# Products of state index 0 scaled on ScalarE instead of VectorE in a selective-scan decoder layer

## The chip, the cores and the metric

The kernel runs on one core of one Trainium2 chip. The metric is the device time of one execution in microseconds, the median of several runs. A core has TensorE (PE: matmuls and transposes into the eight PSUM banks, with PEld for its weight loads), VectorE (DVE), ScalarE (ACT), GpSimd (POOL), and SyncE (SP), which issues the DMAs. Each engine runs its own list of instructions in order and waits on semaphores for the others.

## What is computed

A decoder layer in float32 on 16 sequences of 128 tokens and 1024 features: a selective-scan block, a linear cross-attention and a gated low-rank expert layer, each with residual and layer norm. The change touches the scan alone:

```python
dt = softplus(ts @ W_dt.T + b_dt)
A = -exp(A_log)                              # (2048, 16)
def step(state, inp):
    dt_t, B_t, C_t, u_t = inp
    dA = exp(dt_t[..., None] * A)
    state = state * dA + (dt_t * u_t)[..., None] * B_t[:, None, :]
    y = einsum('bdn,bn->bd', state, C_t)     # sum over the 16 state indices
    return state, y
...
y = ys + x * D
y = y * silu(gate)
return y @ W_out.T
```

## The kernel before

**Tiling.** The 2048 channels are 16 tiles of 128; four sequences (512 tokens) are one group. A step s, of 16, covers one group and a quarter of the channels (4 tiles); q = s % 4 is the quarter. Inside a step the loop runs over the 16 state indices n; U = 16 s + n numbers the units.

**One unit.** GpSimd multiplies dt*u by the row of B of index n into `hb[n % 4]` (L1056). ScalarE writes exp(dt*A) into bank 0 or 1, one tile at a time (L908); for tile i it waits until the scan two tiles earlier has freed that bank. VectorE scans each tile with it (L1143). TensorE transposes the states, four 128x128 pieces for each sequence b (L509, `turn(b)`): sequences 0 and 2 go to bank 2, 1 and 3 to bank 3. Then each bank is multiplied by the column of C (`cg[:, b, n]`) and added to `acc[:, b]`. For sequences 0 to 2 VectorE does this from PSUM in one instruction (`dve_acc`, L1158), or for n=0 as a plain scaled copy (L1155). Sequence 3 goes by ScalarE: a scaled copy (`act_part`, L761), into `acc` for n=0 and into `part` for the other n, where GpSimd adds it (L1013).

**Order.** It is written out by hand. TensorE does for each n: turn 0, turn 1, a share of the filler (projections of Z and X, L432, output products, L456, dt, L444; three 512-column products, each two passes in the trace), turn 2, turn 3, another share. At n=1 and n=11 a product of the next projection into bank 2 (`pe_ssm`, L469) stands behind the third sum. The step ends with transposes of `acc` (L542). VectorE does for each n: sums 0 and 1 of index n, scans 0 and 1 of index n+2, sum 2, scans 2 and 3 of index n+2, then a few odd pieces (`dve_between`); steps 5, 9 and 13 have layer-norm statistics (L1177) there at n=0. At a step's end come the skip and gate products (L1252, L1263), and in steps 4, 8 and 12 then the copy of C's columns into `cg` (L1235). ScalarE does for each n its four exps, with odd pieces between (`act_between`), and then the part of index n-2.

A turn waits until its bank has been read: turns 0, 2 and 3 on `acc_ok` (VectorE's count), turn 1 on `part_ok`.

Of the kernel before, what the change touches and what calls it, by code (L numbers as in the profile page):

```python
# [18 lines left out]
ALU = mybir.AluOpType  # L19
ACT = mybir.ActivationFunctionType  # L20
# [29 lines left out]
OWN = GB - 1  # L50
# [12 lines left out]
def has_x(s):  # L63
    return 0 <= s and LEAD + QD * s < NG * DT
# [29 lines left out]
x_mm conv_base conv_tap conv_done sx_exp sx_ln sx_ok u_ok u_stored0 u_stored1 u_stored2  # L94
ss_mm ss_added ss_square ss_sum ss_mean ss_ln ss_rstd ss_normed bt_mm bt_rows b_stored
wdt_loaded wo_loaded u_loaded0 u_loaded1 r_loaded brep_loaded0 brep_loaded1 brep_loaded2 brep_loaded3
dt_mm dt_abs dt_exp dt_ln dt_ok dtu_ok cg_ok exp_ok bm_ok scan_ok t_done acc_ok part_ok sum_ok yt_mm fin1 fin
z_mm z_copied z_exp z_ln z_sig z_ok o_mm r_added ln_stats ln_aggr ln_eps ln_rstd ln_ok x1_stored
p2_const ones_set ph_mm ph_ok gs_ok cn_loaded ct_loaded x1_loaded xres_loaded out_stored
k_mm k_max k_neg k_exp et_mm et_ok g_mm g_ok rk1 rk2 mt_mm mt_ok  # L100
# [5 lines left out]
def program(nc, a, out):  # L106
# [4 lines left out]
    with ExitStack() as ctx:  # L111
        def sb(name, shape):
            return ctx.enter_context(nc.sbuf_tensor(name, shape, F32))

        S = {name: ctx.enter_context(nc.semaphore(name)) for name in SEMS}

        def after(eng, name, count):

            if count > 0:
                eng.wait_ge(S[name], count)  # L120
# [20 lines left out]
        acc = at(32768, GB, QD * P)  # L141
# [7 lines left out]
        part = at(43520, 2, QD * P)  # L149
# [41 lines left out]
        cg = sb("cg", [P, GB, N])  # L191
# [14 lines left out]
        def bank(i):  # L206
            return banks[i // 2][:, (i % 2) * HALF:(i % 2 + 1) * HALF]
# [289 lines left out]
        def pe_step(pe, s):  # L497
            g, q = divmod(s, NQ)
            for n in range(N):
                U = N * s + n  # L500

                def turn(b):

                    if b == 1:
                        after(pe, "part_ok", U)
                    else:
                        after(pe, "acc_ok", OWN * U + (0, 0, 1, 2)[b])
                    for i in range(QD):
                        last = nc.tensor.transpose(bank(2 + b % 2)[:, i * P:(i + 1) * P],  # L509
                                                   hb[n % 4][:, i * GT + b * P:i * GT + (b + 1) * P],  # L510
                                                   ident[:, :])
                    last.then_inc(S["t_done"], 1)

                pe.wait_ge(S["scan_ok"], QD * (U + 1))
                if n == 2 and (has_x(s - 1) or s == 0):
                    pe.wait_ge(S["ss_added"], (LEAD + QD * s) // 2)
                if n == 4 and q == NQ - 1 and s + 1 < NS:
                    pe.wait_ge(S["bt_rows"], g + 2)
                if n == 12 and has_x(s):
                    pe.wait_ge(S["ss_added"], (LEAD + QD * s) // 2 + 1)  # L520
                turn(0)
                turn(1)
                pe_filler(pe, s, 2 * n)
                turn(2)
                turn(3)
                if n == 1 and (has_x(s - 1) or s == 0):
                    pe.wait_ge(S["acc_ok"], OWN * (U + 1))
                    pe_ssm(pe, (LEAD + QD * s) // 2 - 1)
                if n == 3 and q == NQ - 1 and s + 1 < NS:
                    pe.wait_ge(S["acc_ok"], OWN * (U + 1))  # L530
                    pe_rows(pe, g + 1)
                if n == 11 and has_x(s):
                    pe.wait_ge(S["acc_ok"], OWN * (U + 1))
                    pe_ssm(pe, (LEAD + QD * s) // 2)
                pe_filler(pe, s, 2 * n + 1)

            pe.wait_ge(S["acc_ok"], OWN * N * (s + 1))
            pe.wait_ge(S["sum_ok"], (N - 1) * (s + 1))
            for i in range(QD):
                pe_room(pe, "Y", QD * s + i)  # L540
                for b in range(GB):
                    last = nc.tensor.transpose(home("Y", QD * s + i)[:, b * P:(b + 1) * P],  # L542
                                               acc[:, b, i * P:(i + 1) * P], ident[:, :])
                last.then_inc(S["yt_mm"], 1)
# [200 lines left out]
        def act_ss(act, g):  # L745
# [2 lines left out]
            act.wait_ge(S["ss_ln"], g + 1)  # L748
            nc.scalar.activation(ss3[:, :, :], ss3[:, :, :], ACT.Exp, scale=-0.5).then_inc(S["ss_rstd"], 1)

        def act_part(act, s, n):

            act.wait_ge(S["t_done"], QD * (N * s + n + 1))
            if n == 0:
                after(act, "yt_mm", QD * s)
                act.wait_ge(S["cg_ok"], s // NQ + 1)
                dst = acc[:, OWN, :]
            else:
                after(act, "sum_ok", (N - 1) * s + max(n - 2, 0))
                dst = part[:, n % 2, :]  # L760
            nc.scalar.activation(dst, bank(3), ACT.Identity, scale=cg[:, OWN, n:n + 1])\  # L761
                .then_inc(S["part_ok"], 1)

        def act_between(act, s, n, slot):
# [134 lines left out]
        def act_step(act, s):  # L899
            q = s % NQ  # L900
            for n in range(N):
                U = N * s + n
                for i in range(QD):
                    if n == 0:
                        act.wait_ge(S["dt_ok"], QD * s + i + 1)

                    after(act, "scan_ok", QD * U + i - 1)
                    nc.scalar.activation(by_seq(bank(i % 2))[:, :, 1:SEQ],  # L908
                                         by_seq(dt[s % 2][:, i, :])[:, :, 1:SEQ], ACT.Exp,
                                         scale=a_sb[:, QD * q + i, n:n + 1]).then_inc(S["exp_ok"], 1)  # L910
                    act_between(act, s, n, i)
                if U >= 2:
                    act_part(act, (U - 2) // N, (U - 2) % N)

        def act_keys(act, b, o):
# [90 lines left out]
        def pool_sums(pool, s, n):  # L1006

            if n == 0:
                return
            pool.wait_ge(S["part_ok"], N * s + n + 1)  # L1010
            after(pool, "sum_ok", (N - 1) * s + n - 1)
            v = acc[:, OWN, :]
            nc.gpsimd.tensor_tensor(v, v, part[:, n % 2, :], ALU.add).then_inc(S["sum_ok"], 1)  # L1013
# [131 lines left out]

        def dve_acc(dve, s, n, b):

            k = OWN * (N * s + n) + b
            dve.wait_ge(S["t_done"], QD * (N * s + n) + b + 1)
            c = cg[:, b, n:n + 1]  # L1150
            if n == 0:
                if b == 0:
                    after(dve, "yt_mm", QD * s)
                    dve.wait_ge(S["cg_ok"], s // NQ + 1)
                last = nc.vector.tensor_scalar(acc[:, b, :], bank(2 + b % 2), c, None, ALU.mult)  # L1155
            else:
                dve.wait_ge(S["acc_ok"], k - OWN + 1)
                last = nc.vector.scalar_tensor_tensor(acc[:, b, :], bank(2 + b % 2), c, acc[:, b, :],  # L1158
                                                      ALU.mult, ALU.add)
            last.then_inc(S["acc_ok"], 1)  # L1160

        def dve_out(dve, s, c):

# [66 lines left out]

        def dve_step(dve, s):
            if s % NQ == 0:
                after(dve, "acc_ok", OWN * N * s)
                after(dve, "part_ok", N * s)
                nc.vector.tensor_copy(cg[:, :, :], ssn[:, :, R + N:SS]).then_inc(S["cg_ok"], 1)  # L1235
            for n in range(N):
                U = N * s + n

                for part in range(2):
                    for b in range(2 * part, min(2 * part + 2, OWN)):  # L1240
                        dve_acc(dve, s, n, b)
                    if U + 2 < N * NS:
                        for i in (2 * part, 2 * part + 1):
                            dve_scan(dve, U + 2, i)
                dve_between(dve, s, n)
            if s > 0:
                dve_out(dve, s, 7)

            def skip(i):
                dve.wait_ge(S["yt_mm"], QD * s + i + 1)  # L1250
                d = QD * (s % NQ) + i
                nc.vector.scalar_tensor_tensor(yq[:, i, :], uq[s % 2][:, i, :], dsk[:, d:d + 1],  # L1252
                                               home("Y", QD * s + i), ALU.mult, ALU.add)\
                    .then_inc(S["fin1"], 1)

            after(dve, "o_mm", 8 * s)
            skip(0)
            for i in range(QD):
# [432 lines left out]
```

## Time and profile before

| | |
|---|---|
| median of 3 runs | 3166.69 us (3164.89 to 3166.74) |
| profiled execution | 3165.11 us, span of its instructions 3163.1 us |
| TensorE busy | 2777.4 us (88%) |
| VectorE busy | 2691.1 us (85%) |
| ScalarE busy | 1629.4 us (52%) |
| GpSimd busy | 1850.6 us (59%) |
| mean granted TensorE clock | 0.943 of 2.4 GHz |

Busy shares are means over the whole span. The steps run from about 200 to 2347 us, and the attention and expert part from there to the end. In the rows, a bracket behind a row is the time for which the engine sat idle before it and what released it. A row of a timeline may merge several instructions of one kind.

### The profile page before, as it was taken

What the parts mean: (1) busy time and instruction counts of PE and PEld (TensorE: products, weight loads), DVE (VectorE), ACT (ScalarE), POOL (GpSimd) and SP (SyncE); (2) the same over time, 40 slices, a digit from 0 to 9 for tenths busy, and PEclk for the clock granted to TensorE, in tenths of its full rate; (3) what the DMA queues carried; (4) which work ended last, traced back from release to release, by engine and by line L of the source; (5) the groups of instructions that cost most, each with busy time, mean ns of one, the idle gap of its engine ahead of it and who ended that gap; (6) DMA issues with size and microseconds to landing.
All of it is one profiled execution on the core that took longest, in us unless ns stands there. A gap on an engine that the chain in (4) does not pass through costs nothing.

```text
span 3163.1 us, 34709 instructions
## 1 busy us (share of the span) xinstructions
PE 2777.4 (88%) x10928; PEld 1569.8 (50%) x10928; DVE 2691.1 (85%) x3630; ACT 1629.4 (52%) x2698; POOL 1850.6 (59%) x820
## 2 busy tenths in 40 slices
PE   8967889899978998998988788778887999999996
PEld 4434555455545555554555445444544555555553
DVE  2369999999999999999999999999974877877785
ACT  2346556465545646564555555446533555555553
POOL 1169778687857777785877688678841212221221
PEclk9988999999989999999999898888988999999998
DMA  5442333333242342424233231422202211111110
GB/s 170 131 106 75 100 94 102 118 106 107 89 139 80 102 131 78 126 82 142 80 102 103 63 108 61 128 88 74 67 14 87 73 60 60 53 60 60 60 54 26
DMA packets 132872, 281.27 MB, mean 89 GB/s; under 512 B 12528, under 2 KB 12656, under 8 KB 132224
## 3 DMA queue, kind: packets, MB, share of 16 engines
q1 hardware_dynamic: 132736, 279.59, 28.8%
q8 instruction: 70, 1.15, 0.1%
q14 instruction: 66, 0.54, 0.1%
HBM read 245.86 MB, written 33.69 MB: 88 GB/s over the span
## 4 chain that ended last, share of the span: by engine, by line
PE 49%; DVE 37%; issue 11%; ACT 1%; DMA 0%; POOL 0%; DVEq 0%; SPq 0%; POOLq 0%; ACTq 0%
DVE arena L1143 19%; PE banks L432 15%; DVE arena L1158 8%; PE banks L456 6%; PE banks L509 6%; PE banks L597 3%; PE banks L640 3%; PE banks L553 3%; PE banks L578 3%; PE banks L608 2%; PE banks L469 2%; PE banks L568 1%; DVE arena L1086 1%; DVE rbuf L1171 1%; DVE arena L1252 1%
## 5 line engine op out<-in xcount | busy, mean ns | idle before, releaser
L1056 POOL TENSOR_TENSOR arena<-arena 128x2048 f32<-128x2048 f32 x256 | 1162.8, 4543 | 97.2 <-PE banks L509 97.1
L1143 DVE TENSOR_TENSOR_SCAN arena<-banks,arena 128x512 f32<-128x512 f32 x1024 | 1190.0, 1202 | 9.5 <-POOL arena L1056 9.2
L908 ACT ACTIVATE banks<-arena,a_sb 128x508 f32<-128x508 f32 x1024 | 700.8, 684 | 924.7 <-DVE arena L1143 924.2
L432 PE MATMUL banks<-arena 128*128 128x512 f32 x2048 | 970.2, 613 | 12.3 <-DMA arena<-in_xT 8.1
L509 PE MATMUL banks<-ident,arena 128*128 128x128 f32 x4096 | 593.1, 290 | 214.4 <-DVE arena L1158 134.8
L509 PEld LDWEIGHTS banks<-ident,arena 128*128 128x128 f32 x4096 | 506.8, 149 | 496.5 <-issue 214.6
L1158 DVE SCALAR_TENSOR_TENSOR arena<-banks,cg,arena 128x512 f32<-128x512 f32 x720 | 509.9, 735 | 95.0 <-PE banks L509 94.2
L432 PEld LDWEIGHTS banks<-arena 128*128 128x128 f32 x2048 | 383.2, 199 | 383.0 <-issue 378.1
L1013 POOL TENSOR_TENSOR arena<-arena 128x512 f32<-128x512 f32 x240 | 305.3, 1272 | 395.9 <-ACT arena L761 392.6
L456 PE MATMUL banks<-arena 128*128 128x512 f32 x1024 | 493.7, 620 | 41.0 <-DVE arena L1134 19.7
L1067 POOL TENSOR_TENSOR arena<-arena 128x512 f32<-128x512 f32 x128 | 141.2, 1103 | 458.9 <-DVE arena L1309 458.9
L456 PEld LDWEIGHTS banks<-arena 128*128 128x128 f32 x1024 | 190.9, 200 | 231.6 <-issue 183.6
L1086 DVE SCALAR_TENSOR_TENSOR arena<-banks,taps,arena 128x508 f32<-128x508 f32 (+2 forms) x192 | 141.5, 737 | 121.4 <-ACT arena L696 116.9
L761 ACT ACTIVATE arena<-banks,cg 128x512 f32<-128x512 f32 x256 | 171.3, 669 | 17.1 <-PE banks L509 17.1
L1294 DVE TENSOR_REDUCE arena<-banks 128x8 f32<-128x512 f32 x128 | 88.1, 688 | 102.1 <-PE banks L597 102.1
L1017 POOL TENSOR_TENSOR arena<-arena 128x512 f32<-128x512 f32 x64 | 81.4, 1273 | 148.4 <-ACT arena L710 148.4
L936 ACT ACTIVATE arena<-arena 128x512 f32<-128x512 f32 x128 | 80.7, 631 | 160.4 <-DVE arena L1298 159.8
L597 PE MATMUL banks<-arena 128*128 128x512 f32 x256 | 133.9, 605 | 1.1 <-DVE rbuf L1171 1.1
L553 PE MATMUL banks<-arena 128*128 128x512 f32 x256 | 122.3, 601 | 0.0
L578 PE MATMUL banks<-arena 128*128 128x512 f32 x256 | 120.5, 593 | 0.0
L1076 POOL TENSOR_TENSOR ve<-ve,mhalf 128x1 f32<-128x1 f32 x32 | 17.3, 540 | 174.1 <-DVE ve L1335 174.1
L640 PE MATMUL banks<-arena 128*128 128x512 f32 x256 | 115.1, 593 | 0.7 <-issue 0.7
(130 smaller groups left out, 2813.8 us busy)
## 6 DMA issues: line engine op xcount, KB each, us to landing
arena<-b_scratch SPq DMA_DIRECT2D x128, 512.0 KB, 5.0
arena<-in_WinX SPq DMA_DIRECT2D x128, 256.0 KB, 2.8
arena<-in_WinZ SPq DMA_DIRECT2D x128, 256.0 KB, 2.8
arena<-in_WoutT SPq DMA_DIRECT2D x32, 1024.0 KB, 5.8
u_scratch<-arena SPq DMA_DIRECT2D x64, 256.0 KB, 5.1
arena<-u_scratch SPq DMA_DIRECT2D x16, 1024.0 KB, 9.4
arena<-x_scratch SPq DMA_DIRECT2D x32, 512.0 KB, 3.5
arena<-in_xT SPq DMA_DIRECT2D x14, 1024.0 KB, 7.8
```

The costliest lines, as they stand in the source:

```text
L432: last = nc.tensor.matmul(home(kind, i), wr[w % 2][:, k, :], x[:, k, :], start=(k == 0), stop=(k == KC - 1))
L456: last = nc.tensor.matmul(home("O", i), yq[:, k, b * P:(b + 1) * P], w[:, k, :], start=(k == 0), stop=(k == QD - 1))
L509: last = nc.tensor.transpose(bank(2 + b % 2)[:, i * P:(i + 1) * P], hb[n % 4][:, i * GT + b * P:i * GT + (b + 1) * P], ident[:, :])
L553: last = nc.tensor.matmul(bank(2 + h), wk[:, o * P:(o + 1) * P], cn[:, h * HALF:(h + 1) * HALF], start=True, stop=True)
L578: last = nc.tensor.matmul(bank(6), cT[:, t, :], ekT[:, t, :], start=(t == 0), stop=(t == NT - 1))
L597: nc.tensor.matmul(bank(t % 2), x1[:, t * P:(t + 1) * P], wq, start=True, stop=True)\
L640: last = nc.tensor.matmul(bank(5 + 2 * h), mt[:, o, :], qs[:, o, h * HALF:(h + 1) * HALF], start=(o == 0), stop=(o == OT - 1))
L908: nc.scalar.activation(by_seq(bank(i % 2))[:, :, 1:SEQ], by_seq(dt[s % 2][:, i, :])[:, :, 1:SEQ], ACT.Exp, scale=a_sb[:, QD * q + i, n:n + ...
L1013: nc.gpsimd.tensor_tensor(v, v, part[:, n % 2, :], ALU.add).then_inc(S["sum_ok"], 1)
L1056: nc.gpsimd.tensor_tensor(hb[n % 4].rearrange("p (i t) -> p i t", i=QD), dtu, brep[n // 2 % 4][:, n % 2:n % 2 + 1, :].broadcast_to([P, QD, ...
L1143: nc.vector.tensor_tensor_scan(h, bank(i % 2), h, 0.0, ALU.mult, ALU.add)\
L1158: last = nc.vector.scalar_tensor_tensor(acc[:, b, :], bank(2 + b % 2), c, acc[:, b, :], ALU.mult, ALU.add)
```

## The change

The scaled copies of n=0 of all four sequences are made by ScalarE (`act_first`) straight into `acc`, and VectorE's sums begin at n=1. In ScalarE's order they stand in the slots of n=2: the copy of sequence 0 behind the second exp, of 1 behind the third, of 2 and 3 behind the fourth. A new count, `first_ok`, takes the place of `acc_ok` and `part_ok` where turns and sums wait for a copy of n=0; the other counts are renumbered.

```diff
                 def turn(b):
-                    if b == 1:
-                        after(pe, "part_ok", U)
+                    if n == 0 and b >= 2:
+                        pe.wait_ge(S["first_ok"], GB * s + b - 1)
+                    elif n == 1 and b < 2:
+                        pe.wait_ge(S["first_ok"], GB * s + b + 3)
+                    elif b == 1:
+                        after(pe, "part_ok", (N - 1) * s + max(n - 1, 0))
                     else:
-                        after(pe, "acc_ok", OWN * U + (0, 0, 1, 2)[b])
+                        after(pe, "acc_ok", OWN * (N - 1) * s + OWN * max(n - 1, 0) + (0, 0, 1, 2)[b])
...
+        def act_first(act, s, b):
+
+            act.wait_ge(S["t_done"], QD * N * s + b + 1)
+            if b == 0:
+                after(act, "yt_mm", QD * s)
+                act.wait_ge(S["cg_ok"], s // NQ + 1)
+            nc.scalar.activation(acc[:, b, :], bank(2 + b % 2), ACT.Identity, scale=cg[:, b, 0:1])\
+                .then_inc(S["first_ok"], 1)
...
                     act_between(act, s, n, i)
-                if U >= 2:
+                    if n == 2 and i > 0:
+                        act_first(act, s, i - 1)
+                if n == 2:
+                    act_first(act, s, OWN)
+                elif U >= 2:
                     act_part(act, (U - 2) // N, (U - 2) % N)
...
         def dve_acc(dve, s, n, b):
-            if n == 0:
-                if b == 0:
-                    after(dve, "yt_mm", QD * s)
-                    dve.wait_ge(S["cg_ok"], s // NQ + 1)
-                last = nc.vector.tensor_scalar(acc[:, b, :], bank(2 + b % 2), c, None, ALU.mult)
+            if n == 1:
+                dve.wait_ge(S["first_ok"], GB * s + b + 1)
...
                     for b in range(2 * part, min(2 * part + 2, OWN)):
-                        dve_acc(dve, s, n, b)
+                        if n > 0:
+                            dve_acc(dve, s, n, b)
```

ScalarE at the start of step 1, before (four exps of n=2, then the copy of sequence 3 for n=0):

```order
L761 ACTIVATE arena<-banks,cg 128x512 [waits sum_ok,t_done]
L908 ACTIVATE banks<-arena,a_sb 128x4x127 [waits scan_ok] x4
L761 ACTIVATE arena<-banks,cg 128x512 [waits cg_ok,yt_mm,t_done]
L908 ACTIVATE banks<-arena,a_sb 128x4x127 [waits scan_ok] x4
L761 ACTIVATE arena<-banks,cg 128x512 [waits sum_ok,t_done]
```

The same place in the changed kernel, where the exp is L915, the part L768 and the copy of n=0 L761:

```order
L768 ACTIVATE arena<-banks,cg 128x512 [waits sum_ok,t_done]
L915 ACTIVATE banks<-arena,a_sb 128x4x127 [waits scan_ok] x2
L761 ACTIVATE arena<-banks,cg 128x512 [waits cg_ok,yt_mm,t_done]
L915 ACTIVATE banks<-arena,a_sb 128x4x127 [waits scan_ok]
L761 ACTIVATE arena<-banks,cg 128x512 [waits t_done]
L915 ACTIVATE banks<-arena,a_sb 128x4x127 [waits scan_ok]
L761 ACTIVATE arena<-banks,cg 128x512 [waits t_done] x2
L915 ACTIVATE banks<-arena,a_sb 128x4x127 [waits scan_ok] x4
```

Four copies now stand among and behind the exps of n=2 where one stood behind them.

VectorE at the same step's start, before (scaled copies L1155, scans L1143, sums of n=1 L1158):

```order
L1155 TENSOR_SCALAR arena<-banks,cg 128x512 [waits cg_ok,yt_mm,t_done]
L1155 TENSOR_SCALAR arena<-banks,cg 128x512 [waits t_done]
L1143 SCALAR_TENSOR_TENSOR arena<-banks,arena 128x512 [waits exp_ok,bm_ok]
L1143 SCALAR_TENSOR_TENSOR arena<-banks,arena 128x512 [waits exp_ok]
L1155 TENSOR_SCALAR arena<-banks,cg 128x512 [waits t_done]
L1143 SCALAR_TENSOR_TENSOR arena<-banks,arena 128x512 [waits exp_ok] x2
L1158 SCALAR_TENSOR_TENSOR arena<-banks,cg,arena 128x512 [waits acc_ok,t_done] x2
```

And in the changed kernel (scans L1155, sums L1166):

```order
L1271 TENSOR_TENSOR arena<-arena 128x512 [waits fin1,z_ok] x2
L1155 SCALAR_TENSOR_TENSOR arena<-banks,arena 128x512 [waits exp_ok,bm_ok]
L1155 SCALAR_TENSOR_TENSOR arena<-banks,arena 128x512 [waits exp_ok] x3
L1166 SCALAR_TENSOR_TENSOR arena<-banks,cg,arena 128x512 [waits first_ok,t_done] x2
L1155 SCALAR_TENSOR_TENSOR arena<-banks,arena 128x512 [waits exp_ok,bm_ok]
```

The three scaled copies are gone, and the four scans follow each other directly.

## Rows read from the trace of the kernel before

**Rows 1.** Stretches: busy us and instructions by engine, granted clock, DMA share, GB/s
```profile
core 0: us, PE busy (x) PEld busy (x) DVE busy (x) ACT busy (x) POOL busy (x), PEclk, DMA share, GB/s
200.30:2347.00 2146.70, 1872.26 (x7499) 1083.19 (x7500) 2043.56 (x2322) 1169.85 (x1887) 1645.10 (x618) 0.94 0.32 96
```

**Rows 2.** Timeline of VectorE, start of step 4: start us, us, instruction, idle before
```profile
741.52 1.41 DVE L1155 TENSOR_SCALAR arena<-banks,cg 128x512 f32<-128x512 f32 x2
742.85 2.33 DVE L1143 TENSOR_TENSOR_SCAN arena<-banks,arena 128x512 f32<-128x512 f32 x2
745.09 0.72 DVE L1155 TENSOR_SCALAR arena<-banks,cg 128x512 f32<-128x512 f32 x1
745.74 2.33 DVE L1143 TENSOR_TENSOR_SCAN arena<-banks,arena 128x512 f32<-128x512 f32 x2
748.91 1.41 DVE L1158 SCALAR_TENSOR_TENSOR arena<-banks,cg,arena 128x512 f32<-128x512 f32 x2 [0.85 <-PE banks L509]
...
758.37 1.41 DVE L1158 SCALAR_TENSOR_TENSOR arena<-banks,cg,arena 128x512 f32<-128x512 f32 x2 [2.47 <-PE banks L509]
```

**Rows 3.** Timeline of TensorE, start of step 4
```profile
735.28 2.74 PE L432 MATMUL banks<-arena 128*128 128x512 f32 x6
742.33 1.97 PE L509 MATMUL banks<-ident,arena 128*128 128x128 f32 x8 [4.30 <-DVE arena L1155]
744.09 4.35 PE L432 MATMUL banks<-arena 128*128 128x512 f32 x6
748.28 1.04 PE L509 MATMUL banks<-ident,arena 128*128 128x128 f32 x8
```

**Rows 4.** Who waited for whom over the run: total us, times, longest
```profile
PEld banks L509 <- DVE arena L1155: 71.9, 22, 5.1
DVE arena L1158 <- PE banks L509: 94.2, 101, 3.2
PE banks L509 <- DVE arena L1155: 57.3, 16, 4.3
```

**Rows 5.** Single lines over the run: duration ns min/median/max, first and last start
```profile
L1155 DVE TENSOR_SCALAR arena<-banks,cg x48: 716/734/751, 200.3 to 2245.6; 128x512 f32<-128x512 f32 x48
L761 ACT ACTIVATE arena<-banks,cg x256: 663/668/689, 204.6 to 2347.6; 128x512 f32<-128x512 f32 x128
L1056 POOL TENSOR_TENSOR arena<-arena x256: 4490/4538/4949, 185.5 to 2322.5; 128x2048 f32<-128x2048 f32 x128
```

**Rows 6.** Timeline of ScalarE, start of step 4: exps three and four, the part
```profile
744.10 0.69 ACT L908 ACTIVATE banks<-arena,a_sb 128x508 f32<-128x508 f32 x1 [11.29 <-DVE arena L1143]
745.21 0.69 ACT L908 ACTIVATE banks<-arena,a_sb 128x508 f32<-128x508 f32 x1 [0.43 <-DVE arena L1143]
745.84 0.67 ACT L761 ACTIVATE arena<-banks,cg 128x512 f32<-128x512 f32 x1
```

**Rows 7.** Stretches of step 4 and, last, of step 14; columns as in rows 1
```profile
735.00:738.00 3.00, 3.00 (x11) 1.24 (x8) 3.00 (x2) 0.00 (x0) 2.61 (x1) 1.00 0.22 82
738.00:742.30 4.30, 0.02 (x1) 0.00 (x0) 4.16 (x9) 0.00 (x0) 0.00 (x0) 0.79 0.00 0
742.30:748.30 6.00, 5.97 (x15) 3.47 (x16) 5.76 (x6) 2.88 (x5) 3.86 (x1) 0.58 0.17 56
2120.90:2126.20 5.30, 5.30 (x11) 2.75 (x11) 5.04 (x5) 2.89 (x5) 3.88 (x1) 0.50 0.21 74
```

**Rows 8.** Timelines of VectorE and TensorE, starts of steps 0, 2, 7 and 14
```profile
200.31 1.41 DVE L1155 TENSOR_SCALAR arena<-banks,cg 128x512 f32<-128x512 f32 x2
204.84 1.16 PE L509 MATMUL banks<-ident,arena 128*128 128x128 f32 x8
...
463.76 1.39 DVE L1155 TENSOR_SCALAR arena<-banks,cg 128x512 f32<-128x512 f32 x2
466.32 3.29 PE L432 MATMUL banks<-arena 128*128 128x512 f32 x6
469.45 1.04 PE L509 MATMUL banks<-ident,arena 128*128 128x128 f32 x8
470.22 1.37 DVE L1158 SCALAR_TENSOR_TENSOR arena<-banks,cg,arena 128x512 f32<-128x512 f32 x2
...
1169.16 1.41 DVE L1158 SCALAR_TENSOR_TENSOR arena<-banks,cg,arena 128x512 f32<-128x512 f32 x2 [0.25 <-PE banks L509]
...
2119.41 1.39 DVE L1155 TENSOR_SCALAR arena<-banks,cg 128x512 f32<-128x512 f32 x2
2121.97 4.90 PE L432 MATMUL banks<-arena 128*128 128x512 f32 x6
2126.70 1.04 PE L509 MATMUL banks<-ident,arena 128*128 128x128 f32 x8
2127.34 1.41 DVE L1158 SCALAR_TENSOR_TENSOR arena<-banks,cg,arena 128x512 f32<-128x512 f32 x2 [1.40 <-PE banks L509]
```

**Rows 9.** Timeline of VectorE, start of step 5 with its statistics
```profile
876.21 1.40 DVE L1155 TENSOR_SCALAR arena<-banks,cg 128x512 f32<-128x512 f32 x2
882.65 4.81 DVE L1177 BATCH_NORM_STATS2 st<-rbuf 128x6 f32<-128x512 f32 x8
888.04 1.41 DVE L1158 SCALAR_TENSOR_TENSOR arena<-banks,cg,arena 128x512 f32<-128x512 f32 x2
```

More of the change, by code:

```diff
@@ L96 @@
 wdt_loaded wo_loaded u_loaded0 u_loaded1 r_loaded brep_loaded0 brep_loaded1 brep_loaded2 brep_loaded3
-dt_mm dt_abs dt_exp dt_ln dt_ok dtu_ok cg_ok exp_ok bm_ok scan_ok t_done acc_ok part_ok sum_ok yt_mm fin1 fin
+dt_mm dt_abs dt_exp dt_ln dt_ok dtu_ok cg_ok exp_ok bm_ok scan_ok t_done first_ok acc_ok part_ok sum_ok yt_mm fin1 fin
 z_mm z_copied z_exp z_ln z_sig z_ok o_mm r_added ln_stats ln_aggr ln_eps ln_rstd ln_ok x1_stored
@@ L526, in pe_step @@
                 if n == 1 and (has_x(s - 1) or s == 0):
-                    pe.wait_ge(S["acc_ok"], OWN * (U + 1))
+                    pe.wait_ge(S["acc_ok"], OWN * ((N - 1) * s + n))
                     pe_ssm(pe, (LEAD + QD * s) // 2 - 1)
                 if n == 3 and q == NQ - 1 and s + 1 < NS:
-                    pe.wait_ge(S["acc_ok"], OWN * (U + 1))
+                    pe.wait_ge(S["acc_ok"], OWN * ((N - 1) * s + n))
                     pe_rows(pe, g + 1)
                 if n == 11 and has_x(s):
-                    pe.wait_ge(S["acc_ok"], OWN * (U + 1))
+                    pe.wait_ge(S["acc_ok"], OWN * ((N - 1) * s + n))
                     pe_ssm(pe, (LEAD + QD * s) // 2)
                 pe_filler(pe, s, 2 * n + 1)
-            pe.wait_ge(S["acc_ok"], OWN * N * (s + 1))
+            pe.wait_ge(S["acc_ok"], OWN * (N - 1) * (s + 1))
             pe.wait_ge(S["sum_ok"], (N - 1) * (s + 1))
@@ L749, in act_ss @@
             nc.scalar.activation(ss3[:, :, :], ss3[:, :, :], ACT.Exp, scale=-0.5).then_inc(S["ss_rstd"], 1)
+        def act_first(act, s, b):
[5 more added lines that the diff above has]
+                .then_inc(S["first_ok"], 1)
         def act_part(act, s, n):
             act.wait_ge(S["t_done"], QD * (N * s + n + 1))
-            if n == 0:
[L755 to L761, printed above, removed]
+            after(act, "sum_ok", (N - 1) * s + max(n - 2, 0))
+            nc.scalar.activation(part[:, n % 2, :], bank(3), ACT.Identity, scale=cg[:, OWN, n:n + 1])\
                 .then_inc(S["part_ok"], 1)
@@ L1009, in pool_sums @@
                 return
-            pool.wait_ge(S["part_ok"], N * s + n + 1)
+            pool.wait_ge(S["part_ok"], (N - 1) * s + n)
+            pool.wait_ge(S["first_ok"], GB * (s + 1))
             after(pool, "sum_ok", (N - 1) * s + n - 1)
@@ L1146, in dve_acc @@
         def dve_acc(dve, s, n, b):
-            k = OWN * (N * s + n) + b
+            k = OWN * ((N - 1) * s + n - 1) + b
             dve.wait_ge(S["t_done"], QD * (N * s + n) + b + 1)
-            c = cg[:, b, n:n + 1]
-            if n == 0:
-                if b == 0:
-                    after(dve, "yt_mm", QD * s)
-                    dve.wait_ge(S["cg_ok"], s // NQ + 1)
-                last = nc.vector.tensor_scalar(acc[:, b, :], bank(2 + b % 2), c, None, ALU.mult)
+            if n == 1:
+                dve.wait_ge(S["first_ok"], GB * s + b + 1)
             else:
                 dve.wait_ge(S["acc_ok"], k - OWN + 1)
-                last = nc.vector.scalar_tensor_tensor(acc[:, b, :], bank(2 + b % 2), c, acc[:, b, :],
-                                                      ALU.mult, ALU.add)
-            last.then_inc(S["acc_ok"], 1)
+            nc.vector.scalar_tensor_tensor(acc[:, b, :], bank(2 + b % 2), cg[:, b, n:n + 1], acc[:, b, :],
+                                           ALU.mult, ALU.add).then_inc(S["acc_ok"], 1)
         def dve_out(dve, s, c):
@@ L1232, in dve_step @@
             if s % NQ == 0:
-                after(dve, "acc_ok", OWN * N * s)
-                after(dve, "part_ok", N * s)
+                after(dve, "acc_ok", OWN * (N - 1) * s)
+                after(dve, "part_ok", (N - 1) * s)
                 nc.vector.tensor_copy(cg[:, :, :], ssn[:, :, R + N:SS]).then_inc(S["cg_ok"], 1)
```

## The prediction

> **What bounds the kernel now.** I read the page first, then the busy time by part of the program, then who waits for whom, and last the timelines of three engines around one step boundary. The program has a state-space part (16 steps of 16 indices n) and an attention and expert part. The step loop runs from 200.3 to about 2347 us, and the change touches nothing outside it. There VectorE is busy 2043.56 of 2146.70 us (95%) and TensorE 1872.26 us, while ScalarE has 977 us free [rows 1]. By shares alone one would take work from VectorE and give it to ScalarE. That is an average, so the next question is which wait ends last where the work is taken away.
>
> The place is the start of a step. VectorE has finished the previous step, TensorE has turned products 0 and 1 of n=0 into banks 2 and 3 and has run its filler. Banks 2 and 3 are the only two for turned products, so turn 2 waits until product 0 has been read, turn 3 until product 1 has been read. In step 4 TensorE sits idle 4.30 us for the first scaled copy and then needs 1.97 us for turns 2 and 3, 4.35 us for the filler, and only then makes the turns of n=1 [rows 3]. VectorE, in the same stretch, reaches the sums of n=1 and waits 0.85 us for TensorE, and 2.47 us again at n=2 [rows 2]. So from the first scaled copy to the sums of n=1 the chain is: product 1 read, turn 3, filler, turn 0 of n=1, sum. VectorE's scans lie beside that chain, not on it. Over the run VectorE waits 94.2 us for the turns, in 101 places, and TensorE's wait for the scaled copies is 57.3 us in 16 places, one for each step [rows 4].
>
> **What is removed.** 48 scaled copies, three a step, with a median of 734 ns [rows 5]. Instructions overlap a little: the pair takes VectorE from 741.52 to the scan at 742.85, that is 1.33 us, and the third from 745.09 to 745.74, 0.65 us [rows 2]. So a step frees 1.98 us of VectorE and the run 31.7 us. This is the gain if VectorE is the bound at that place.
>
> **What is added.** 48 ScalarE copies of 668 ns each [rows 5], 32 us of an engine that has 977 us free. Their cost is not their length but their place in ScalarE's order. The copy of product 0 stands behind the second exp of index 2, which ran long before: ScalarE is idle for 11.29 us before the third exp [rows 6]. It is done as soon as turn 0 is, so turn 2 no longer waits (except in steps 4, 8 and 12, where the row of C is copied on VectorE just ahead; there it runs about as now). The copy of product 1 stands behind the third exp, and that exp waits for the first scan of the new step to free its bank. Call A the time at which VectorE begins the step's n=0 work. Now: A is 741.52 and turn 3 may start when the second scaled copy has ended, at A+1.41, in fact near A+1.5. After: the scan starts at A, the third exp 1.25 us after the scan does (742.85 to 744.10), the next ScalarE instruction 0.63 us later (745.21 to 745.84), and it takes 0.67 us [rows 2, 6]. With 0.05 us for the signal, turn 3 starts at A+2.60. **Turn 3 comes 1.1 us later than now**, although VectorE does less. The wait has moved from an instruction at the head of VectorE's queue to one that is behind a scan and an exp.
>
> Queued behind turn 3 on TensorE are the filler and the turns of n=1, and VectorE's sums of n=1 wait for those. VectorE itself is ready for them at A+4.5 and idles. The other new waits end in time: copies of products 2 and 3 end near A+3.9 and A+4.6, and the turns of n=1 that need them come after A+5. The fourth exp still ends (A+3.25) before its scan can start (A+3.5). GpSimd's product for n=4 waits for turn 3 too; at 4.54 us [rows 5] it would be done near A+8, and its scans come after the sums of n=2, at A+16.8 in step 4. The SyncE queue waits on none of the changed counts; its transfers are moved with TensorE's filler.
>
> **The clock.** The granted clock was 1.00 for the filler before the idle stretch, and 0.58 from 742.3 to 748.3, after the 4.3 us without work [rows 7]. The filler took 2.74 us where the clock was 1.00 and 4.35 us here; it took 3.29 us in step 2 and 4.90 us in step 14, where the grant was 0.50 throughout [rows 3, 7, 8]. From the start of turn 3 (A+1.5) to the first turn of n=1 that makes 3.1 us at 2.4 GHz (step 0: A is 200.31, the turn 204.84) and 5.8 us at 1.2 GHz (step 14: 2119.41 and 2126.70) [rows 8]. In the twelve steps that hang on this chain it lies between 4.2 us (step 2: 463.76 and 469.45) and those 5.8 us; step 4 has 5.2, and the mean that I take for the twelve is 4.7 [rows 2, 3, 8]. After the change TensorE is idle from about A-2.9 to A+2.60, 5.5 us instead of 4.3, so the fall comes before work is taken up again and, as the rise in these rows comes only after work has gone on for some us, more of the chain runs at 1.2 GHz. I take 5.3 us, midway between today's mean and the 5.8 of step 14, the one step that had 1.2 GHz all the way.
>
> The Trainium skill, "TensorE: Matmul & The Clock Gate", section "HAM oscillation — how this bites in real kernels", says that a wait of a few us between short bursts drops the array to half rate, and that each following burst then starts cold. The trace agrees in the direction (0.58 after 4.3 us of idleness); read strictly, the page would put the whole chain at half rate, which is my upper end.
>
> **The sum.** For twelve steps (1 to 4, 6 to 8, 10 to 12, 14, 15) the sums of n=1 start about 0.65 us after the first turn of n=1 does (748.28 to 748.91; 2126.70 to 2127.34), now on average near A+6.85. After: 2.60 + 5.3 + 0.65 = A+8.55, which is 1.7 us later. Bounds: with today's 4.7 us it is A+7.95, 1.1 us later; with 5.8 us A+9.05, and a little behind that for the turns themselves, 2.2 us later. What follows hangs on these sums: VectorE works without a break from there, and where it waits again (2.47 us at n=2) TensorE is itself waiting for the third sum of n=1, so the shift is passed on to the end of the step. 12 x 1.7 = +20.4 us (13 to 26).
> For steps 5, 9 and 13 VectorE has 5.4 us of statistics between the scans and the sums of n=1, which start at A+11.84 without a wait [rows 9]. After, VectorE is ready at A+9.86 and TensorE at about A+8.55. These keep the whole gain, 3 x -1.98 = -5.9 us.
> Step 0 has no wait at n=1 and about 1.1 us of slack against turn 3 coming later at full clock: +0.2 to +1.5, I take +0.5.
> Together +15 us (+7 to +22). The profiled execution took 3165.11 us (span 3163.1); that gives 3180, and the median of the runs shown, 1.6 us higher, 3181.7. I forecast 3181 us.
>
> **Rivals.**
> - VectorE is the bound after all: if turn 3 came no later, or TensorE's filler had slack, each step would gain its 1.98 us, 16 x 1.98 = 31.7, down to 3135 us; half of it, 3151, if only half of the steps behave as step 5 does. For it: 95% busy, and a wait of only 0.25 us in step 7 and none in step 2 [rows 8]. Against it: a wait that is small now only says that both chains end together, and one of them grows. It decides from where VectorE reaches the sums of n=1 later than TensorE does, about A+8.5, which only the three steps with statistics do. Chance 0.10.
> - The clock keeps its present share: the same mechanism with 4.7 us, +7 us, 3174 us; chance 0.25. This straddles what counts as no change.
> - The chain lengthens and the low clock also holds for the turns and the filler after it, so that the third sum of n=1 waits as well: 12 x 2.6 - 5.9 + 1.5 = +27 us, 3194 us. It decides where the clock rises later than A+8. Chance 0.12.
> - Other low-clock stretches elsewhere shift by chance and cancel the loss: near 3167 us, chance 0.08.
> - My forecast, 3181 us: chance 0.45.
>
> **How the numbers follow.** A measurement of this kernel can tell about 0.2% from no change, 6.3 us, so 3160.4 to 3173.0 counts as same. Faster holds the first rival, 0.10. Same holds the chance rival and part of the second, 0.17. Slower holds the rest, 0.73. The range of 8 in 10 reaches from 3167 (the second rival's lower side) to 3194.
>
> **What would show it.** Right: TensorE's idle time before turn 3 ends on a ScalarE copy and turn 3 starts 2.6 us after the first scan of the step; VectorE waits 3 to 4.5 us before the sums of n=1 in twelve steps, none in steps 5, 9 and 13; granted clock between turn 3 and the turns of n=1 near 0.5 to 0.6. Wrong: VectorE's wait there stays under 2 us, or turn 3 starts before A+1.5, or steps other than 5, 9 and 13 become shorter.

## The result, and the profile after

| | before | changed |
|---|---|---|
| median of 20 runs | 3164.86 us (3159.69 to 3166.74) | 3172.89 us (3169.35 to 3175.95) |
| span of the profiled execution | 3163.1 us | 3170.2 us |
| mean granted TensorE clock | 0.943 | 0.941 |

The changed kernel takes 1.0027 times as long, with a 95% interval of 1.002 to 1.0034: slower by 8 us. VectorE is busy 30 us less, and the time grew.

The page of the changed kernel, busy us by engine, and below it two rows of who waited for whom (total us, times, longest) and one of a single line (VectorE's sums):

```profile
PE 2776.5 (88%) x10928; PEld 1563.9 (49%) x10928; DVE 2660.6 (84%) x3582; ACT 1655.8 (52%) x2746; POOL 1851.1 (58%) x820
DVE arena L1166 <- PE banks L513: 138.7, 102, 4.6
PE banks L513 <- ACT arena L761: 76.1, 20, 5.3
L1166 DVE SCALAR_TENSOR_TENSOR arena<-banks,cg,arena x720: 720/741/753, 206.8 to 2357.9; 128x512 f32<-128x512 f32 x180
```

These answer to [rows 4, 5]. VectorE's wait for the turned products went from 94.2 to 138.7 us, and TensorE's wait for a scaled copy is now one for ScalarE's (L761), 76.1 us instead of 57.3. The last sum of the steps starts at 2357.9 us; before it was 2347.2. So the steps became 10.7 us longer, and what follows them 3.6 us shorter.

One step's start in the changed kernel, step 2, on ScalarE, TensorE and VectorE (L915 exp, L761 copy of n=0, L513 turns, L432 filler, L1155 scans, L1166 sums), and the stretch's busy times with the granted clock:

```profile
467.89 0.69 ACT L915 ACTIVATE banks<-arena,a_sb 128x508 f32<-128x508 f32 x1 [6.71 <-DVE arena L1155]
468.52 0.67 ACT L761 ACTIVATE arena<-banks,cg 128x512 f32<-128x512 f32 x1
```
```profile
469.24 1.12 PE L513 MATMUL banks<-ident,arena 128*128 128x128 f32 x4 [5.33 <-ACT arena L761]
470.15 5.16 PE L432 MATMUL banks<-arena 128*128 128x512 f32 x6
475.14 1.04 PE L513 MATMUL banks<-ident,arena 128*128 128x128 f32 x8
```
```profile
466.65 4.55 DVE L1155 TENSOR_TENSOR_SCAN arena<-banks,arena 128x512 f32<-128x512 f32 x4
475.78 1.41 DVE L1166 SCALAR_TENSOR_TENSOR arena<-banks,cg,arena 128x512 f32<-128x512 f32 x2 [4.58 <-PE banks L513]
```
```profile
469.30:475.00 5.70, 5.70 (x10) 2.77 (x11) 1.90 (x2) 2.95 (x5) 4.49 (x1) 0.50 0.25 86
```

A is 466.65. The copy of product 1 stands behind the third exp, which began when the first scan had freed its bank, and turn 3 starts at 469.24, A+2.59. TensorE had been idle 5.33 us, and the turn and the filler after it ran at 0.50, 1.2 GHz. The first turn of n=1 comes at A+8.49 and the sums at A+9.13; in [rows 8] they came at A+5.69 and A+6.46. VectorE waits 4.58 us where it waited for nothing.

### The profile page after: what moved, and what is told of

It is laid out like the page before. It is cut to its first block, busy times and chain, and to the rows that moved or that the text cites. A ratio compares the mean times of both kernels' runs of the same rounds, so it can differ in the third digit from the quotient of the medians.

```text
span 3170.2 us, 34709 instructions
## 1 busy us (share of the span) xinstructions
PE 2776.5 (88%) x10928; PEld 1563.9 (49%) x10928; DVE 2660.6 (84%) x3582; ACT 1655.8 (52%) x2746; POOL 1851.1 (58%) x820
## 4 chain that ended last, share of the span: by engine, by line
PE 50%; DVE 36%; issue 11%; ACT 2%; DMA 1%; POOL 0%; DVEq 0%; SPq 0%; POOLq 0%; ACTq 0%
DVE arena L1155 19%; PE banks L432 17%; DVE arena L1166 8%; PE banks L456 6%; PE banks L513 6%; PE banks L601 3%; PE banks L644 3%; PE banks L557 3%; PE banks L582 3%; PE banks L612 2%; PE banks L469 2%; PE banks L572 2%; DVE arena L1098 1%; DVE rbuf L1178 1%; DVE arena L1260 1%
## 5 line engine op out<-in xcount | busy, mean ns | idle before, releaser
L1155 DVE TENSOR_TENSOR_SCAN arena<-banks,arena 128x512 f32<-128x512 f32 x1024 | 1189.9, 1205 | 9.5 <-POOL arena L1068 9.2
L915 ACT ACTIVATE banks<-arena,a_sb 128x508 f32<-128x508 f32 x1024 | 699.1, 684 | 853.4 <-DVE arena L1155 852.9
L432 PE MATMUL banks<-arena 128*128 128x512 f32 x2048 | 986.5, 622 | 12.3 <-DMA arena<-in_xT 8.1
L513 PE MATMUL banks<-ident,arena 128*128 128x128 f32 x4096 | 588.4, 287 | 225.0 <-DVE arena L1166 126.6
L513 PEld LDWEIGHTS banks<-ident,arena 128*128 128x128 f32 x4096 | 502.5, 148 | 508.0 <-issue 226.9
L1166 DVE SCALAR_TENSOR_TENSOR arena<-banks,cg,arena 128x512 f32<-128x512 f32 x720 | 511.1, 738 | 139.3 <-PE banks L513 138.7
L432 PEld LDWEIGHTS banks<-arena 128*128 128x128 f32 x2048 | 387.4, 201 | 389.8 <-issue 384.4
L456 PE MATMUL banks<-arena 128*128 128x512 f32 x1024 | 488.8, 615 | 41.1 <-DVE arena L1146 20.4
L768 ACT ACTIVATE arena<-banks,cg 128x512 f32<-128x512 f32 x240 | 160.5, 669 | 16.8 <-PE banks L513 16.5
```

The source lines that it names most:

```text
L432: last = nc.tensor.matmul(home(kind, i), wr[w % 2][:, k, :], x[:, k, :], start=(k == 0), stop=(k == KC - 1))
L456: last = nc.tensor.matmul(home("O", i), yq[:, k, b * P:(b + 1) * P], w[:, k, :], start=(k == 0), stop=(k == QD - 1))
L915: nc.scalar.activation(by_seq(bank(i % 2))[:, :, 1:SEQ], by_seq(dt[s % 2][:, i, :])[:, :, 1:SEQ], ACT.Exp, scale=a_sb[:, QD * q + i, n:n + ...
L1155: nc.vector.tensor_tensor_scan(h, bank(i % 2), h, 0.0, ALU.mult, ALU.add)\
```

## Experiments

Times are compared as ratios to the kernel before, measured on the same chip.

**Delay turn 3 and change nothing else** (late_copy, on the kernel before):

```diff
                     for b in range(2 * part, min(2 * part + 2, OWN)):
+                        if n == 0 and b == 1:
+                            dve_scan(dve, U + 2, 0)
                         dve_acc(dve, s, n, b)
                     if U + 2 < N * NS:
                         for i in (2 * part, 2 * part + 1):
-                            dve_scan(dve, U + 2, i)
+                            if n > 0 or i > 0:
+                                dve_scan(dve, U + 2, i)
```

> The kernel before (all copies of n=0 for sequences 0 to 2 on VectorE), with one thing moved: VectorE makes the copy of product 1 behind its first scan instead of ahead of it. VectorE does as much as before, and turn 3 comes at about A+2.6 as in the changed kernel. Theory A: turn 3's time alone sets the twelve steps, so the sums of n=1 come 1.5 to 2 us later in them and nothing is gained in steps 5, 9 and 13: 15 to 25 us over the kernel before, 3180 to 3190 us. Theory B: VectorE's load and TensorE's volume are unchanged, so within 3 us of the kernel before.

Measured: 3185.31 us, ratio 1.0069 (1.0056 to 1.0083), +21 us. TensorE and VectorE at the start of step 2:

```profile
468.77 1.12 PE L509 MATMUL banks<-ident,arena 128*128 128x128 f32 x4 [1.12 <-DVE arena L1155]
469.67 5.11 PE L432 MATMUL banks<-arena 128*128 128x512 f32 x6
```
```profile
466.20 0.74 DVE L1155 TENSOR_SCALAR arena<-banks,cg 128x512 f32<-128x512 f32 x1
475.26 1.41 DVE L1158 SCALAR_TENSOR_TENSOR arena<-banks,cg,arena 128x512 f32<-128x512 f32 x2 [2.53 <-PE banks L509]
```

Turn 3 at A+2.57 and the sums at A+9.06, with VectorE's work the same as before and no copy moved to ScalarE. The place of the copy of product 1 alone accounts for a loss of this kind and size.

**Keep TensorE busy in the gap** (warm, on the changed kernel):

```diff
+                    if n == 0 and b == 2 and s % NQ:
+                        for _ in range(6):
+                            nc.tensor.matmul(bank(2), ident[:, :], hb[0][:, 0:GT], start=True, stop=True)
                     for i in range(QD):
                         last = nc.tensor.transpose(bank(2 + b % 2)[:, i * P:(i + 1) * P],
```

> The changed kernel with six extra 512-column products into the free bank 2 ahead of turn 2, in the twelve steps where s % 4 is not 0; their result is overwritten by the turn and used by nothing. They fill TensorE's idle stretch, so that the granted clock stays at 2.4 GHz. Theory A with a price on the clock: turn 3 still starts at A+2.6, the first turn of n=1 at A+5.7 instead of about A+8.3, the sums at A+6.3: nine steps 2.0 to 2.6 us shorter, 18 to 24 us under the changed kernel, about 3151 us. If the delay of turn 3 alone were the cost and the clock nothing: no difference from the changed kernel (within 3 us).

Measured: 3162.03 us, ratio 0.9996 (0.9987 to 1.0005); the changed kernel has 1.0027, so about 10 us are gained. Step 2, TensorE, VectorE and the stretch:

```profile
460.59 5.31 PE L514 MATMUL banks<-arena,ident 128*128 128x512 f32 x12
...
466.52 0.66 PE L516 MATMUL banks<-ident,arena 128*128 128x128 f32 x4 [0.18 <-ACT arena L764]
467.02 2.74 PE L432 MATMUL banks<-arena 128*128 128x512 f32 x6
```
```profile
470.23 1.41 DVE L1169 SCALAR_TENSOR_TENSOR arena<-banks,cg,arena 128x512 f32<-128x512 f32 x2 [1.75 <-PE banks L516]
```
```profile
466.40:469.50 3.10, 2.98 (x10) 1.59 (x11) 2.08 (x2) 3.03 (x6) 2.17 (x1) 1.00 0.09 14
```

Turn 3 still starts at A+2.59, but the granted clock is 1.00, the filler takes 2.74 us instead of 5.16, and the sums come at A+6.30 instead of A+9.13. So of the distance from A to the sums 2.8 us in this step was the low clock, brought on by idleness. The gain of 10 us is less than the 18 to 24 expected: steps 5 and 9 each became 3.2 us longer, because TensorE, further ahead there, waited 1.4 us in front of turn 2 of n=1 instead of not at all and then ran slowly (VectorE's wait at n=2 grew from 2.47 to 4.0 us). In steps 1, 14 and 15 the six products ended after the copy was ready, so turn 3 came only at A+3.1 to A+3.3.

**Take the exp out of the way of the copy** (early1, on the changed kernel), and **all four copies ahead of the third exp** (all_early). The diff is that of early1; all_early makes the copies of all four sequences in a row behind the second exp.

```diff
                     if n == 2 and i > 0:
-                        act_first(act, s, i - 1)
-                if n == 2:
-                    act_first(act, s, OWN)
-                elif U >= 2:
+                        for b in ((0, 1), (2,), (OWN,))[i - 1]:
+                            act_first(act, s, b)
+                if n != 2 and U >= 2:
```

> The changed kernel with one thing moved: ScalarE's copy of product 1 stands directly behind that of product 0, ahead of the third exp (2 behind the third exp, 3 behind the fourth). Theory A (the loss is the wait of turn 3 on a copy that stands behind a scan and an exp): turn 3 starts before the step's first scan, VectorE's 3.5 to 4.6 us of waiting before the sums of n=1 fall to 0, and each step keeps its 1.98 us; 31.7 us under the kernel before, about 3133 us (3128 to 3142), 40 us under the changed kernel. Theory B (TensorE has no time to give in a step, so VectorE's freed time is worth little wherever the copies stand): 3155 to 3165 us.

> The changed kernel with all four copies directly behind the second exp of n=2. Theory A: as with only product 1 moved, and in twelve steps no difference, since VectorE has its scans to do anyway; in steps 4, 8 and 12 the copies begin only when C's columns are copied, so the third exp comes up to 1.5 us late and the third scan waits some 1 us: 3 to 5 us slower than the version with only product 1 moved, about 3137 us. Theory B: 3155 to 3165 us.

Measured: 3183.42 us, ratio 1.007 (1.0056 to 1.0083), and 3202.62 us, ratio 1.0124 (1.0109 to 1.014). Both expectations failed, theory B's as much as theory A's. The end of step 1 and the start of step 2 in early1, on VectorE (L1270 gate products, L1154 scans, L1165 sums) and GpSimd (L1067):

```profile
465.05 4.93 DVE L1270 TENSOR_TENSOR arena<-arena 128x512 f32<-128x512 f32 x2
469.91 4.55 DVE L1154 TENSOR_TENSOR_SCAN arena<-banks,arena 128x512 f32<-128x512 f32 x4
474.38 1.38 DVE L1165 SCALAR_TENSOR_TENSOR arena<-banks,cg,arena 128x512 f32<-128x512 f32 x2
```
```profile
464.06 4.77 POOL L1067 TENSOR_TENSOR arena<-arena 128x2048 f32<-128x2048 f32 x1 [1.40 <-PE banks L513]
```

The sums of n=1 follow the scans with no wait, at A+4.47, as theory A said. But the last two gate products take 4.93 us; in the changed kernel the same pair takes 1.28. The first of them lasts 4.33 us and ends at 469.38, 0.55 us behind the end of GpSimd's product for n=4 (464.06 + 4.77 = 468.83). That product waits for turn 3 only, and turn 3 now comes while VectorE is still in the gate products. Twelve step ends lose 3.65 or 4.3 us each, 46 us, more than the 32 us that are gained. It does not show as a wait: VectorE is counted as busy. A smaller loss comes on top: in step 2 TensorE had been idle 6.10 us before the turns of n=1, its filler then took 4.03 us, and the third sum of n=1 waited 1.09 us for it.

In all_early TensorE also runs so far ahead that it waits 5.21 us before turn 2 of n=1, and the product in front of the sums of n=2 (L469), 2.02 us in the changed kernel, takes 3.73:

```profile
479.57 1.97 PE L513 MATMUL banks<-ident,arena 128*128 128x128 f32 x8 [5.21 <-DVE arena L1165]
483.11 3.73 PE L469 MATMUL banks<-arena 128*128 128x96 f32 x16 [1.58 <-DVE arena L1165]
```

**Hold GpSimd back until the gate products are done** (early1_hold4 and early1_hold3 on early1, before_hold3 on the kernel before, after_hold3 on the changed kernel; the number is the n whose product waits):

```diff
                 after(pool, "t_done", QD * (U - 3))
+                if n == 4:      # or 3
+                    after(pool, "fin", QD * s)
```

> The version early1 with one wait added on GpSimd: its product for n=4 starts only when VectorE has finished the gate products of the step before. In early1 that product started under VectorE's last two gate products, which then took 4.93 us instead of 1.28. Theory C (the lost gain of early1 is VectorE waiting for GpSimd on two-SBUF-input instructions at the step's end): twelve step ends 3.65 us shorter, 44 us under early1, about 3139 us. Theory D (early1's loss is TensorE's earlier order and its clock): within 5 us of early1, 3180 us.

Measured: 3140.86 us, ratio 0.9927 (0.9913 to 0.994), 43 us under early1. Theory C holds: the gate products take 47 us less than in early1 over the run. The same place:

```profile
462.06 1.28 DVE L1272 TENSOR_TENSOR arena<-arena 128x512 f32<-128x512 f32 x2
463.27 4.55 DVE L1156 TENSOR_TENSOR_SCAN arena<-banks,arena 128x512 f32<-128x512 f32 x4
467.74 1.38 DVE L1167 SCALAR_TENSOR_TENSOR arena<-banks,cg,arena 128x512 f32<-128x512 f32 x2
```
```profile
463.52 4.51 POOL L1069 TENSOR_TENSOR arena<-arena 128x2048 f32<-128x2048 f32 x1 [3.85 <-DVE arena L1272]
```

> The kernel before with one wait added on GpSimd: its product for n=3 starts only when VectorE has finished the gate products of the step before. Theory C: the first gate product takes 0.7 us instead of 3.07, 2.4 us for each of fifteen step ends, and TensorE's idle stretch is as much shorter, so its clock falls less; 36 to 42 us under the kernel before, about 3126 us. Theory D: no change, or slower if the late product holds up a scan.

Measured: 3138.77 us, ratio 0.9915 (0.9901 to 0.9929): 25 us gained, not 36 to 42. The gate products over the whole run (ns, min/median/max), first in the kernel before, then here:

```profile
L1263 DVE TENSOR_TENSOR arena<-arena x64: 675/678/3523, 323.3 to 2356.1; 128x512 f32<-128x512 f32 x64
```
```profile
L1265 DVE TENSOR_TENSOR arena<-arena x64: 681/683/687, 321.6 to 2330.1; 128x512 f32<-128x512 f32 x64
```

The kernel before had the same collision at the end of every step but the last. Its first gate product ran under GpSimd's product for n=3; at the end of step 1, on VectorE and GpSimd:

```profile
457.65 3.07 DVE L1263 TENSOR_TENSOR arena<-arena 128x512 f32<-128x512 f32 x1
```
```profile
455.63 4.54 POOL L1056 TENSOR_TENSOR arena<-arena 128x2048 f32<-128x2048 f32 x1
```

Here too the product on VectorE ends 0.55 us behind the one on GpSimd (460.72 and 460.17). Held back, no gate product takes over 0.69 us, and the granted clock is 1.00 between turn 3 and the turns of n=1 in all sixteen steps. The mechanism is as expected, the size is not. The stretched products had cost 33 us and not 36, since four of the fifteen took 2.0 to 2.9 us only. Steps 2, 6 and 10 became 2.34 us shorter, but steps 5 and 9 only 1.4, as the wait before the sums of n=2 grew from 3.2 to 4.15 us there.

> The changed kernel (product 1's copy behind the third exp) with GpSimd's product for n=3 held until VectorE has finished the gate products, as in before_hold3. Theory C: fifteen step ends 2.4 us shorter, 36 us under the changed kernel. Theory A with the clock: TensorE's idle stretch ahead of turn 3 begins 2.4 us later, so it is short enough for the clock to stay at 2.4 GHz, turn 3 still starts at A+2.6, the first turn of n=1 at A+5.7 and the sums at A+6.35, just where VectorE reaches them in before_hold3 (A+6.46): the change then costs nothing in twelve steps and gains 1.98 us in three, 3132 us (3128 to 3136), under before_hold3 (3138.8). If the clock falls all the same: sums near A+8, 3150 to 3158 us, above before_hold3.

Measured: 3124.53 us, ratio 0.9889 (0.9872 to 0.9905), under before_hold3's 0.9915, with intervals that just overlap. TensorE and VectorE in step 3:

```profile
594.22 0.66 PE L513 MATMUL banks<-ident,arena 128*128 128x128 f32 x4 [2.95 <-ACT arena L761]
594.71 2.74 PE L432 MATMUL banks<-arena 128*128 128x512 f32 x6
```
```profile
591.62 4.56 DVE L1157 TENSOR_TENSOR_SCAN arena<-banks,arena 128x512 f32<-128x512 f32 x4
597.92 1.41 DVE L1168 SCALAR_TENSOR_TENSOR arena<-banks,cg,arena 128x512 f32<-128x512 f32 x2 [1.74 <-PE banks L513]
```

Turn 3 is as late as in the changed kernel (A+2.60), but after 2.95 us of idleness the filler takes 2.74 us and the sums come at A+6.30. Of the twelve steps five do so; in five the sums come at A+8.0 and in two at A+9.2, because the clock fell all the same. The time is that of the better branch (the ratio makes it 3129 us where the kernel before takes 3164), but not by its mechanism, for in seven steps the sums are later than in before_hold3. Step by step against before_hold3, the twelve steps together are as long as there; the gain is in steps 5, 9 and 13, which are 5.4, 5.1 and 3.2 us shorter, because TensorE waits 0, 1.4 and 2.3 us in front of turn 2 of n=1 where it waited 4.4, 4.4 and 5.3. With the idle stretch shorter, the same change no longer loses; that it gains is likely, but the intervals overlap.

> early1 with the wait at n=3, which holds back both products. Theory C: 2.4 us for each of fifteen step ends below early1_hold4, 3103 us, a little less where TensorE's clock stays up (3095 to 3106). Theory D: 3180 us.

Measured: 3102.47 us, ratio 0.9803 (0.9789 to 0.9816). The size is as expected, its spread over the steps is not: steps 5, 9, 13 and 14 did not become shorter, the others by 1.8 to 4.1 us. Against before_hold3, which has the same wait on GpSimd, the change with copies 0 and 1 side by side is worth 36 us; without that wait the same version lost 19.

**Copy C's columns ahead of the skip and gate products** (early1_hold3_cg, on early1_hold3):

```diff
             if s > 0:
                 dve_out(dve, s, 7)
+            if (s + 1) % NQ == 0 and s + 1 < NS:
+                dve.wait_ge(S["acc_ok"], OWN * (N - 1) * (s + 1))
+                dve.wait_ge(S["part_ok"], (N - 1) * (s + 1))
+                nc.vector.tensor_copy(cg[:, :, :], ssn[:, :, R + N:SS]).then_inc(S["cg_ok"], 1)
```

The copy at the start of a step is left for step 0 alone (that part of the diff is not shown).

> early1_hold3 with the copy of C's columns in steps 4, 8 and 12 made ahead of the skip and gate products instead of behind them. Then these three steps lose the wait of 3.05 us before the sums of n=1 that they have in early1: 9 us under early1_hold3, about 3092 us. If the wait comes from elsewhere: no difference.

Measured: 3098.37 us, ratio 0.9794 (0.9781 to 0.9808). The three steps have their sums at A+4.48 as expected, but the difference of 4 us from early1_hold3 lies within the intervals. There was less to gain than the 9 us expected: the waits of about 3.05 us were those of early1, and in early1_hold3 they were 2.36, 2.37 and 0.67 us. The start of step 2:

```profile
453.16 1.29 DVE L1274 TENSOR_TENSOR arena<-arena 128x512 f32<-128x512 f32 x2
454.37 4.56 DVE L1156 TENSOR_TENSOR_SCAN arena<-banks,arena 128x512 f32<-128x512 f32 x4
458.85 1.39 DVE L1167 SCALAR_TENSOR_TENSOR arena<-banks,cg,arena 128x512 f32<-128x512 f32 x2
```

These two are the fastest versions: the change with copies 0 and 1 side by side and GpSimd held back is 2% faster than the kernel before.

## Why the prediction was right, and what it mis-sized

**Place of the copy, turn 3 at A+2.60.** Right: A+2.59 in every step. The kernel before had it at A+1.60 on average over the twelve steps, not A+1.5, so it came 1.0 us later and not 1.1. late_copy shows that this alone costs 21 us. The other signs came as written: VectorE waits 3.4 to 4.6 us before the sums of n=1 in twelve steps and not at all in steps 5, 9 and 13, and the granted clock between turn 3 and the turns of n=1 is 0.51 to 0.64 in the twelve.

**Sums of n=1 later in twelve steps, 1.7 us each.** Right in kind, a little low: they come on average at A+8.7 instead of A+6.86, +1.85 us, 22 us in all against 20.4. The clock's part of it was real. From turn 3 to the first turn of n=1 the twelve steps took 4.6 us on average, at a granted clock of 0.67, and now take 5.5 us at 0.56; warm shows what it is worth. So the rival in which the clock keeps its share is refuted. Step 14, from which the upper bound was read, did not move: its clock had been low before, and its sums went from A+7.93 to A+8.00.

**Steps 5, 9 and 13 keep 1.98 us each.** This term was mis-sized. Step 13 gained 2.2 us, but steps 5 and 9 gained 4.4 each, so the three gave 11 us instead of 5.9. TensorE's passage from turn 2 of n=1 to the filler ahead of the turns of n=2 in step 5, before and then after, with the granted clock of the stretch (L509 and L513 are the turns):

```profile
888.85 1.31 PE L509 MATMUL banks<-ident,arena 128*128 128x128 f32 x8 [3.06 <-DVE arena L1158]
892.39 3.73 PE L469 MATMUL banks<-arena 128*128 128x96 f32 x16 [2.23 <-DVE arena L1158]
895.91 3.56 PE L432 MATMUL banks<-arena 128*128 128x512 f32 x6
```
```profile
892.00:899.90 7.90, 7.51 (x28) 5.55 (x29) 3.13 (x4) 3.97 (x7) 6.74 (x3) 0.65 0.02 6
```
```profile
895.42 1.04 PE L513 MATMUL banks<-ident,arena 128*128 128x128 f32 x8
898.09 2.02 PE L469 MATMUL banks<-arena 128*128 128x96 f32 x16 [1.63 <-DVE arena L1166]
899.95 2.77 PE L432 MATMUL banks<-arena 128*128 128x512 f32 x6
```
```profile
899.90:905.00 5.10, 5.10 (x20) 2.81 (x20) 2.63 (x5) 2.25 (x4) 5.10 (x3) 1.00 0.23 72
```

Before, TensorE had stood idle 3.06 us in front of turn 2 of n=1 in this step, and the clock fell to 0.65 over the chain behind it. In the changed kernel TensorE arrives later and VectorE earlier, the idleness in front of turn 2 is gone, and the two rows behind it take 2.5 us less. The prediction counted the clock at one place of the step only; the same delay that cost clock behind turn 3 gave it back behind turn 2. warm and before_hold3 show the reverse: where TensorE got ahead, VectorE's wait at n=2 in steps 5 and 9 grew again, to 4.0 and 4.15 us.

**"What follows is passed on."** Nearly. The twelve steps grew by 21.3 us, step 0 by 0.2 (I had taken 0.5), and the three with statistics shrank by 11.0: with 0.2 us ahead of the first step the steps end 10.7 us later against the +15 of the sum. Steps 5 and 9 with their 5 us are the difference. In steps 2, 6 and 10 the shift of about 2.5 us shrinks to about 1 us by the end of the step (in step 2 a low-clock stretch near n=7, 0.72 before, is gone); in steps 11, 12 and 15 it grew by 0.7 to 1.7 us.

**Outside the steps** I had counted nothing. From the last sum to the end it took 812.3 us instead of 815.9, with the same code. The difference is TensorE's clock at two places, about 19 us and 749 us behind the end of the steps; the same two stretches, before and then changed:

```profile
2375.70:2395.70 20.00, 8.81 (x22) 5.67 (x23) 3.72 (x7) 0.00 (x0) 0.00 (x0) 0.50 0.68 199
3105.90:3109.50 3.60, 3.60 (x12) 2.41 (x11) 1.94 (x5) 2.09 (x4) 1.55 (x2) 0.53 0.00 0
```
```profile
2386.40:2406.40 20.00, 9.61 (x27) 6.15 (x28) 3.85 (x7) 0.90 (x1) 0.00 (x0) 0.57 0.67 203
3116.60:3120.20 3.60, 3.60 (x24) 2.68 (x23) 2.11 (x4) 2.42 (x5) 2.06 (x2) 1.00 0.03 7
```

The clock rose some 3 us earlier in the first and did not fall in the second. The profiles of the other runs have 812.2 or 812.3 us there (early1, after_hold3, early1_hold3_cg), 814.8 (early1_hold3) or 816.0 to 816.8, whatever the change. What chooses between them is open. The prediction has no term for it.

**Luck.** The forecast was +15 us; the medians grew by 8.0 and the profiled executions by 7.1. Of the 7.9 us that the latter lack, 4.3 lie in the steps and 3.6 behind them. Against the median that the prediction started from (3166.69 us, three runs) the changed kernel is only 6.2 us longer, just inside the 3160.4 to 3173.0 that the prediction itself called no change; that the twenty runs of each side tell the two apart is what makes it slower. The number nearest to the measured one, 3174 us, belongs to the rival whose mechanism did not occur. So direction and mechanism are borne out by late_copy, warm and the signs, and the size is right only within the wide range.

**GpSimd.** The prediction asked when its product for n=4 is needed, found room, and stopped. It did not ask on whom it would fall if it came earlier. In the changed kernel the product for n=4 did no harm, since turn 3 came later; the one for n=3 still stretched a gate product to 3.07 us, as before. The collision is the main reason why the obvious mending, early1, lost 19 us. The trace of the kernel before had shown it: one gate product of 3.07 us among others of 0.68.

**Rival 1, VectorE is the bound after all.** Its gain of 31.7 us (3135 us) was within reach, but only with two obstacles away, the place of the copy and GpSimd's product. early1_hold4 has no wait at n=1 in nine of the twelve steps and measured 3141 us; from before_hold3 to early1_hold3 the same moved work gained 36 us.

## To carry to other kernels

When work moves to an idle engine, ask behind which instruction it will stand and what that one waits for; a copy of 0.67 us that stands behind a scan and an exp delayed its reader by 1.0 us on average, and TensorE's low clock after that idleness made it 1.85 us. When the profile shows one instruction of a line several times as long as its sisters, look at what the neighbour engine ran at that moment before moving anything: a stall of this kind counts as busy time and appears in no list of waits. Holding the neighbour back by one semaphore wait, here GpSimd until the gate products were done, gained 25 us on the kernel before, and it turned the best version of the change from a loss of 19 us into a further gain of 36.

## What the runs showed of the hardware

A product of two SBUF operands on VectorE and GpSimd's own product on SBUF did not run side by side. A gate product of 0.68 us took 3.07 us under one of GpSimd, and a pair took 4.93 us under another. Of the gate products that began under a GpSimd product, all 15 in the kernel before and 27 of 28 in early1 ended 0.55 us behind its end. The other way round, 11 GpSimd products of early1 that began under a gate product took 4.71 to 5.00 us instead of 4.54. VectorE's scans and sums, which read one operand from PSUM, ran beside the same GpSimd product at their usual 1.20 and 0.74 us; of some 750 that lay wholly under one in the kernel before, no scan took over 1.23 us and no sum over 0.76. The Trainium skill, "SBUF — State Buffer", section "SBUF: two separate sides", says that VectorE and GpSimd share one pair of ports, taken as an exclusive lock for a whole instruction, and that a VectorE instruction with two SBUF inputs takes part in this. The traces agree: with GpSimd held back the longest of 64 gate products fell from 3523 to 687 ns.

TensorE's granted clock was 0.50 after 5.33 us of idleness in step 2 of the changed kernel, and a filler of 2.74 us took 5.16 us behind it. In after_hold3 eleven of the sixteen steps have the same 2.95 us of idleness before turn 3: behind it the clock fell in seven (2, 5, 6, 7, 10, 11, 15) and stayed at 1.00 in four (3, 9, 13, 14); step 8, with 1.83 us of idleness before turn 2 and 1.00 us before turn 3, had 0.50. In before_hold3, where TensorE stood idle at most 1.92 us before turn 2, it stayed at 1.00 up to the turns of n=1 in every step. Six useless products in the gap (5.31 us) made the changed kernel about 10 us faster than without them.
